# Dense keys and 64-row score products in a six-layer windowed attention block on one core

## The reference, cut to what matters

```
q, k, v = heads(shift(x) @ Wqkv)           # 16 heads of 64
q = rotate(l2norm(q) * qs, scale);  k = rotate(l2norm(k) * ksc, 1 / scale)
for each window w of 32 queries:           # 16 windows in 512 tokens
    keys = the 32 of window w-1 and the 32 of window w
    sim  = (q @ keys.T) * 8, masked to key <= query <= key + 32
    out  = softmax(sim) @ values
x = out @ Wo + x
x = (a * gelu(gate)) @ W2 + b2 + x         # a, gate from layernorm(shift(x)) @ W1 + b1
```

## Time and profile before

| | us |
|---|---|
| median of 3 runs (4729.05 to 4734.5) | 4732.04 |
| the profiled execution | 4724.0 |
| its span | 4722.2 |
| PE busy | 4365.8 |
| DVE busy | 3863.2 |
| ACT busy | 2967.2 |
| POOL busy | 2807.6 |

### The profile page before, as it was taken

How to read it: one execution, slowest core, us unless ns; L and a number is a source line. 1 busy time by engine, 2 the same in 40 slices (tenths; PEclk the granted TensorE clock), 3 DMA queues, 4 the chain that set the end, 5 groups by cost and what they waited for, 6 DMA issues and landing times. The chain is left out here.

```text
span 4722.2 us, 102300 instructions
## 1 busy us (share of the span) xinstructions
PE 4365.8 (92%) x36584; PEld 3032.7 (64%) x36584; DVE 3863.2 (82%) x5311; ACT 2967.2 (63%) x4089; POOL 2807.6 (59%) x4591
## 2 busy tenths in 40 slices
PE   5999999999789999999999999999999999999996
PEld 3555555555467776776777776776766776776775
DVE  6888888888678888888888888888888888888884
ACT  4666666666356666666666666666666666666663
POOL 3555555555466666566566666666666666666663
PEclk9999999999899999999999999999999999999999
DMA  1000000000110011110110011110011110110010
GB/s 52 4 4 5 5 3 5 2 5 2 46 30 25 25 29 36 38 30 23 27 50 26 26 29 27 45 33 24 25 33 43 27 31 23 27 52 25 25 30 14
DMA packets 256459, 119.24 MB, mean 25 GB/s; under 512 B 118337, under 2 KB 251457, under 8 KB 255169
## 3 DMA queue, kind: packets, MB, share of 16 engines
q1 hardware_dynamic: 256192, 115.87, 8.9%
HBM read 86.31 MB, written 16.91 MB: 22 GB/s over the span
## 5 line engine op out<-in xcount | busy, mean ns | idle before, releaser
L579 POOL TENSOR_TENSOR pn<-es,rden 128x1024 f32<-128x1024 f32 x192 | 366.2, 1907 | 693.4 <-DVE rden L911 693.4
L673 ACT ACTIVATE y<-ps 128x1024 f32<-128x1024 f32 x384 | 372.1, 1021 | 642.0 <-PE ps L1112 642.0
L861 DVE TENSOR_TENSOR t<-ps,tabl 128x1024 f32<-128x1024 f32 x384 | 468.0, 1219 | 252.0 <-ACT sq L693 251.2
L563 POOL TENSOR_TENSOR t<-t,ardn 128x1024 f32<-128x1024 f32 x256 | 484.6, 1893 | 300.5 <-DVE ardn L796 300.1
L583 POOL TENSOR_TENSOR t<-t 128x1024 f32<-128x1024 f32 x192 | 454.1, 2365 | 311.6 <-DVE t L863 311.5
L664 ACT ACTIVATE t<-ps,anm,srn 128x512 f32<-128x512 f32 x512 | 392.5, 770 | 275.9 <-DVE anm L805 275.9
L863 DVE TENSOR_TENSOR t<-ps,tabl 128x512 f32<-128x512 f32 x768 | 490.5, 680 | 0.0
L960 DVE TENSOR_TENSOR qn<-t,rn 128x2048 f32<-128x2048 f32 x192 | 439.0, 2286 | 62.1 <-POOL rn L388 62.0
L1112 PE MATMUL ps<-pT,xw 64*128 64x256 f32 x3072 | 384.8, 390 | 82.9 <-DVE x L932 79.3
L585 POOL TENSOR_TENSOR t<-t 128x1024 f32<-128x1024 f32 x192 | 455.4, 2372 | 0.0
L989 PEld LDWEIGHTS ps<-cst,qn 128*128 128x128 f32 x3072 | 342.0, 141 | 160.1 <-DVE qn L960 87.8
(11 more groups left out here) (135 smaller groups left out, 9192.9 us busy)
## 6 DMA issues: line engine op xcount, KB each, us to landing
xw<-tokens_dram SPq DMA_DIRECT2D x768, 64.0 KB, 1.9
tokens_dram<-x SPq DMA_DIRECT2D x96, 128.0 KB
xs<-tokens_dram SPq DMA_DIRECT2D x192, 64.0 KB, 1.9
xsh<-x SPq DMA_DIRECT2D x48, 128.0 KB
xsh<-x SPq DMA_DIRECT2D x48, 127.0 KB
wm<-in_l_wqk SPq DMA_DIRECT2D x3, 1024.0 KB, 5.2
wv<-in_l_wv SPq DMA_DIRECT2D x6, 512.0 KB, 4.0
wo<-in_l_wo SPq DMA_DIRECT2D x6, 512.0 KB, 5.4
```

The source lines that it names most:

```text
L563: nc.gpsimd.tensor_tensor(eA[:, v], eA[:, v], ardn[:, v].unsqueeze(2).to_broadcast([P, 2, SEQ]), ALU.mult).then_inc(a_pn, 1)
L861: nc.vector.tensor_tensor(t13, q3, tabl[:, 0, u, i].unsqueeze(1).to_broadcast([P, H, DH]), ALU.mult)
```

## The change

Keys are stored densely: `kT` holds, for each of 8 pairs, 544 columns with the even head in rows 0 to 63 and the odd head in rows 64 to 127, with no zeros. One ACT copy of 128 x 1024 fills it where two of 64 x 1024 filled `kpad`. The scores of one head and one window are a matmul of 64 rows and 32 columns against 64 keys: 64 matmuls in place of 32. Even heads use the upper 64 rows of the array and write one PSUM bank, odd heads the lower 64 and the next bank. The scores, and all that follows, so stand with even heads first, and the output matmul takes its weights as `h` where it took `slot(h)`. POOL's memset shrinks from 128 x 8704 to 128 x 256 elements.

```
-        kpad = sb("kpad", [P, H, WIN + SEQ])
+        kbuf = sb("kbuf", [P, 4 * NU * SEQ])
+        kT = kbuf[:, 0:PAIRS * (WIN + SEQ)].rearrange("p (a c) -> p a c", a=PAIRS)
-            nc.gpsimd.memset(kpad[:], 0.0).then_inc(s_zero, 1)
+            nc.gpsimd.memset(kT[:, :, 0:WIN], 0.0).then_inc(s_zero, 1)
-                    act.activation(*keys(0, (c + 2) % NU), ACT.Copy)
-                    act.activation(*keys(1, (c + 2) % NU), ACT.Copy).then_inc(l_kT, 1)
+                    u = (c + 2) % NU
+                    act.activation(kT[:, :, WIN + u * P:WIN + (u + 1) * P], pool2.rearrange("p (a c) -> p a c", a=PAIRS),
+                                   ACT.Copy).then_inc(l_kT, 1)
-                            m = nc.tensor.matmul(ps_o, y[:, h], mhL[s.v][:, slot(h)], start=(h == 0), stop=(h == H - 1))
+                            m = nc.tensor.matmul(ps_o, y[:, h], mhL[s.v][:, h], start=(h == 0), stop=(h == H - 1))
                     for a in range(PAIRS):
-                        for w in range(NW):
-                            key0 = u * P + w * WIN
-                            m = nc.tensor.matmul(pool1[w * WIN:(w + 1) * WIN, a * 2 * KEYS:(a + 1) * 2 * KEYS],
-                                                 qT[:, a, w * WIN:(w + 1) * WIN], kpad[:, 2 * a:2 * a + 2, key0:key0 + KEYS],
-                                                 start=False, stop=True, skip_group_check=True)
+                        for odd in range(2):
+                            rows = slice(odd * DH, (odd + 1) * DH)
+                            for w in range(NW):
+                                key0 = u * P + w * WIN
+                                m = nc.tensor.matmul(pool1[w * WIN:(w + 1) * WIN, odd * 512 + a * KEYS:odd * 512 + (a + 1) * KEYS],
+                                                     qT[rows, a, w * WIN:(w + 1) * WIN], kT[rows, a, key0:key0 + KEYS],
+                                                     start=False, stop=True, skip_group_check=True)
```

More of the change, by code:

```diff
@@ L178, in build @@
         wqkA = wqkL[0].rearrange("p (a c) -> p a c", a=PAIRS)
+        kT = kbuf[:, 0:PAIRS * (WIN + SEQ)].rearrange("p (a c) -> p a c", a=PAIRS)
         eA = t12[:].rearrange("p (j s k) -> p j s k", j=NU, s=2)
-        pTA = kpad[:].rearrange("p h c -> p (h c)")[:, 0:4 * NU * SEQ].rearrange("p (v s k q) -> p v s k q", v=2, s=2, k=NU)
+        pTA = kbuf[:, 0:4 * NU * SEQ].rearrange("p (v s k q) -> p v s k q", v=2, s=2, k=NU)
         qkA = qn[:].rearrange("p (v u c) -> p v u c", v=2, u=NU)
@@ L317, in build @@
         s_out = sem("s_out")
[L319 to L323, removed]
         def layers(eng, turn):
```

## The result

| | before | after |
|---|---|---|
| median of 4 runs, us | 4732.05 (4729.05 to 4734.5) | 4762.43 (4757.68 to 4768.92) |
| profiled execution, us | 4724.0 | 4757.68 |
| its span, us | 4722.2 | 4755.8 |
| mean granted clock | 0.992 | 0.983 |
| PE busy, us | 4365.8 | 4321.7 |

The changed kernel is slower: the ratio is 1.0062, with an interval of 1.0049 to 1.0076. The forecast said 0.99, and its range ended at 4738.

A forecast was written before the change was run, and what follows sets the result against it. DVE-POOL ring bounds 83 turns, DVE's L932 51, scores 58. From 4724.0, minus 46 (products) and 1 (copies), gives 4677 profiled; 8.0 more makes the median 4685 us, range 4674 to 4738.

The forecast's parts named there:

- three kinds of turn: Of 192 turns, 83 bound by a ring through DVE and POOL, 51 by DVE's L932, 58 by the scores.
- The copies: ACT's key copies, two made one: 1.02 us less ACT work a turn, outside the ring; gain 1 us in all.
- the memset: POOL's one-time zeroing before the layers, 7.35 us cut to a fraction of one; gain 0, bounds 0 and 1.
- no change: Rival for the score products: eight tiles do not run at once; median 4731 to 4738 us, chance 0.16.
- The 0.80 us: Gain of the score products in each c = 1 turn, at 0.056 us a step; 46 us over 58 turns.
- lower bound of 0.45: Least gain of the score products, in us a turn, if the 32-column weight load is not hidden behind the columns.
- the 58 waits of L950: DVE's L950 waiting for the scores in 58 turns, taken as the only turns where earlier scores save time.
- the starts set the pace: Rival for the score products: 28 ns a record, 128 records taking 3.55 us; median 4961 us, chance 0.11.
- point of decision, 13 ns: Start pace per record from which 128 score records take as long as the 64 before.
- the clock: Rival in c = 0 turns: longer PE idle lowers the clock, 1.6 us a fall, 83 us; median 4768, chance 0.04.
- covered by the wait for L932: In 51 turns (c = 0) PE waits for DVE's L932 anyway, so earlier scores gain nothing.
- over half of: Share of the 51 c = 0 turns needing a clock fall for the change to become a loss.

The follow-up runs named there:

- even-heads kernel: The changed kernel with only the even heads' scores computed, 32 products of 64 rows a turn instead of 64; 4737.28 us (one run).

## Why the prediction was wrong

**Right.** There are three kinds of turn, and only c = 1 has the scores in its chain: c = 2 stayed at 16.81, c = 0 without a fall at 18.38, and an ordinary c = 1 turn kept all that the products gained (row 0.47 shorter, turn 0.47 shorter). Of DVE's wait for the scores, 77.2 us, 46.2 are left. The copies were worth nothing that can be measured, and the layers' first transposes start at 1263.1 us where they started at 1263.0, so the memset was not either. Row halves and column quarters do work at the same time, eight tiles in 56 ns, and the rival "no change" fell with that. PE waited for DVE's addition in 126 turns, not 51:

```profile
PE ps L1108 <- DVE x L928: 136.4, 126, 2.6
```

**A term mis-sized: the gain of the products.** The 0.80 us were "since nothing is left over at that pace". The pace of 56 ns for eight holds for 32 records of 128; then it is 10.7 ns a record, not 7. The gain is 0.47 us, near the lower bound of 0.45, but not for that bound's reason (an unhidden weight load): the even-heads kernel has the same loads and keeps to 56 ns a group. With 58 x 0.47 = 27 us in place of 46 the forecast would have been 4704. The count was too high as well: not all of the 58 waits of L950 lie in ordinary c = 1 turns, and 38 turns by 0.47 are 18 us. (The slack ahead of L960 is 0.40 us by the rows, not 0.38; nothing hangs on that.) The rival "the starts set the pace" named this mechanism. It took 28 ns a record as the price, from bursts of four, and that was the wrong end: the four records of a burst had waited for columns. Its own point of decision, 13 ns, was not reached. A sentence on the rule of about 25 ns between two starts (the Trainium skill, page "TensorE: Matmul & The Clock Gate", section "Wait — 56ns, not 53.3ns?") stood beside it in the prediction. The trace does not bear the rule out for matmuls on different tiles: they start 7 ns apart in a burst and 10.7 ns apart on average after it.

**A chance mis-set: the clock.** The rival was right in kind and nearly in size (1.6 us a fall, measured 1.64), with a chance of 0.04. That its 4768 lies near the 4762 is luck: it took a fall in every turn, a gain of 46 us and no cost of the jumps. The prediction had the warning: an idle time that grows past 1.78 us, and two layer ends with 3.1 to 3.2 us of idle, of which one brought a fall (in the whole trace it is three of five, with 2.75 to 3.21 us). No row showed what 2.2 to 2.6 us do, but one in two was the rate that the rows gave, and for 51 turns it gives 41 us. The sum left it out, since the idle time of c = 0 was booked as cover ("covered by the wait for L932"). That cover had a price of its own. It was also said that the sign turns in "over half of" the turns; with a gain of 27 us it turns at 17 of them.

**A term missing: the jump back.** "PE gets 32 more matmuls a turn; if they start at the pace above, that is in the sum." It is not: they also lengthen the loop's program, and 24 jumps cost 21 us. No row of before shows such a wait, and the row of the instruction queue, 2.39 MB, was not read. It could not have told the limit, but a bound was to be had by adding the loop's growth to the list of unknown prices.

By terms, for the profiled execution: forecast 4677; slower pace +19, fewer turns +9, falls +42, jumps +21, the waits at three ends of layers -9.5: 4758.5; measured 4757.7. (What else there is, some 5 us more behind the last turn and small differences of the other sign, nearly cancels.) The median lies 4.8 us above it and not 8.0.

## What to carry to other kernels

Idle time of TensorE that "covers" a gain is not free: here the clock began to fall behind waits of about 2 us, and the work behind them then took nearly twice as long, so shorten the wait (here by moving one independent DVE step) in the same edit that makes PE faster. Count the instructions that a hardware loop's body gets, not only their time, and look for waits with no releaser behind the jump; the instruction queue's bytes say that a body is read again, but straight code moves as many without a wait. Many small matmuls on separate tiles gain until the feed sets the pace, so measure a burst longer than what may be queued before the pace of its first records is used in a sum.

## What the runs showed of the hardware

- Eight tiles (two row halves, four column quarters) work at once: eight float32 records of 64 columns in 56 ns. Beyond the first 32 records the pace is 10.7 ns a record, and 9.8 with 32 columns.
- A batch loop whose body grew by 128 instructions a turn is read again at each jump: 11 packets more, and the turn ahead of it 0.7 to 1.3 us longer. With 64 more a turn it is not. Written out as straight code, 372 packets in all cause no such wait.
- Of 48 recurring waits of PE the granted clock fell behind none at 1.78 us, behind 20 at 2.09, 26 at 2.23 and 38 at 2.43. At ends of layers in the kernel before it fell behind three waits of five (2.75 to 3.21 us).
- Even without the reading, the loop's form costs: written out, c = 0 is 0.26 and c = 3 0.14 us shorter in the kernel before.
